# Building the one-hot matrices of an edge aggregation on VectorE (one equality compare) instead of ScalarE (distance and ramp)

## What is computed

```python
msgs = concatenate([h[src], edge_attr_64], axis=-1)     # 100000 x (256 + 64)
msgs = silu(msgs @ W + b)                               # W: 320 x 256
out = segment_sum(msgs, dst, num_segments=3125)         # sum of the messages of each node
out = layernorm(out, eps=1e-3) * gamma + beta
x = x + out
```

## Time and profile before

| | |
|---|---|
| median of 3 executions | 7204.5 us |
| the profiled execution | 7204.5 us, span 7202.7 us |
| mean granted clock of TensorE | 0.81 of full speed |
| busy share of the span: PE, PEld, DVE, ACT, POOL | 67%, 49%, 71%, 55%, 68% |
| the stage of the change | about 4826 to 5862 us of the span |

### The profile page before, as it was taken

The page is one execution under the profiler, slowest core; times in us unless marked ns, Lnnn a source line. Parts: engine busy times, 40 slices in busy tenths (PEclk is TensorE's granted clock), DMA queues, the critical chain, the costliest instruction groups (busy, mean ns, idle before and its releaser), DMA issues. The chain is left out here.

```text
span 7202.7 us, 124927 instructions
## 1 busy us (share of the span) xinstructions
PE 4843.2 (67%) x21121; PEld 3517.2 (49%) x21122; DVE 5093.3 (71%) x11748; ACT 3926.9 (55%) x9134; POOL 4916.3 (68%) x4990
## 2 busy tenths in 40 slices
PE   5463157777726777766777777769999971677775
PEld 4353135555514555544555555546666651444443
DVE  7665267777747777787888888875555564777777
ACT  4342157777626777752444444437777751666664
POOL 0376677777567777757777777767777762777773
PEclk9855578888867888888988888879999975778877
DMA  5422244444414444534666666634444432454443
GB/s 175 49 69 46 68 125 136 135 135 136 106 46 135 134 135 136 137 88 133 181 182 176 180 179 179 184 79 131 131 131 131 131 79 69 134 136 137 136 135 86
DMA packets 625331, 906.00 MB, mean 126 GB/s; under 512 B 345945, under 2 KB 399862, under 8 KB 624794
## 3 DMA queue, kind: packets, MB, share of 16 engines
q0 software_dynamic: 248160, 655.67, 33.4%
q1 hardware_dynamic: 376666, 223.78, 12.2%
q10 hardware_dynamic: 416, 25.60, 1.1%
HBM read 869.74 MB, written 61.59 MB: 129 GB/s over the span
## 5 line engine op out<-in xcount | busy, mean ns | idle before, releaser
L1444 POOL DMA_INDIRECT at_ring<-tab_s,at_idx x816 | 774.2, 949 | 310.6 <-issue 204.6
L1924 POOL DMA_INDIRECT ad_ring<-tab_qv,ad_idx x816 | 780.1, 956 | 274.9 <-issue 213.1
L1444 POOL DMA_INDIRECT at_ring_0a<-tab_s,at_idx_0a x816 | 778.4, 954 | 273.5 <-issue 204.5
L1444 POOL DMA_INDIRECT at_ring_0b<-tab_s,at_idx_0b x816 | 777.2, 952 | 273.2 <-issue 205.4
L2305 POOL DMA_INDIRECT ae_ring<-tab_a,ae_idx x816 | 771.3, 945 | 257.6 <-issue 232.9
L1603 PE MATMUL at_po<-at_rows,at_hot 128*128 128x260 f32 x1632 | 562.5, 504 | 109.6 <-DVE at_begin L103 82.3
L2124 PE MATMUL ad_pk<-node_a,ad_hr 128*128 x1632 | 479.4, 445 | 217.4 <-DVE ad_prod L1996 119.1
L1603 PE MATMUL at_po_0b<-at_rows_0b,at_hot_0b 128*128 128x264 f32 x1632 | 510.2, 466 | 113.3 <-DVE at_begin_0b L103 95.9
L1603 PE MATMUL at_po_0a<-at_rows_0a,at_hot_0a 128*128 128x264 f32 x1632 | 505.9, 463 | 114.3 <-DVE at_begin_0a L103 100.4
L575 POOL DMA_INDIRECT recs_s<-rnk_recs_now,rnk_pos_now x294 | 286.6, 975 | 360.3 <-DVE rnk_both L478 272.1
L2199 ACT ACTIVATE ad_hot<-iota_row,ad_nrel 128x128 f32<-128x128 f32 x816 | 259.0, 388 | 487.9 <-PE ad_po L2143 487.9
(11 more groups left out here) (503 smaller groups left out, 12726.9 us busy)
## 6 DMA issues: line engine op xcount, KB each, us to landing
at_rr_0a<-relrow_d SPq DMA_DIRECT2D x102, 256.0 KB
at_rr_0b<-relrow_d SPq DMA_DIRECT2D x102, 256.0 KB
ad_rr<-relrow_d SPq DMA_DIRECT2D x102, 256.0 KB
ae_feat<-attr_pad SPq DMA_DIRECT2D x816, 32.0 KB
at_rr<-relrow_s SPq DMA_DIRECT2D x102, 256.0 KB
rnk_lrow<-lorow_f SPq DMA_DIRECT2D x98, 256.0 KB
attr_pad<-in_edge_attr_dram ACTq DMA_DIRECT2D x1, 25000.0 KB, 79.5
at_ring_0a<-tab_s,at_idx_0a POOLq DMA_INDIRECT x816
```

The source lines that it names most:

```text
L1444: eng.indirect_dma_start(out=ring[:, t.slot * STEP + u, :], out_offset=None, in_=table, in_offset=bass.IndirectOffsetOnAxis(ap=idx[:, t.sl ...
L1924: eng.indirect_dma_start(out=ring[:, t.slot * STEP + u, :], out_offset=None, in_=table, in_offset=bass.IndirectOffsetOnAxis(ap=idx[:, t.sl ...
```

## The change

The one-hot matrices move from ACT to DVE. `prepare(q)` now first issues one `tensor_tensor` with `is_equal` over the quad (128 x 512), whose inputs are `iota_row`, repeated 4 times, and the positions `rel_sb`, each repeated 128 times; both lie in SBUF. ACT's function `one_hots`, its copy of `nrel` and the semaphore `far` are gone, five instructions for each quad and one for each turn. `load_columns` brings `rel` in place of `nrel`. DVE has 24 counted instructions in a turn, before 20, and the counts that PE and ACT wait for follow that; each still stands for the same `pre`. The wait of `add` for `summed` is the same but for an offset.

```diff
-        per = QUAD * 5
-        pre_at = {0: 0, 1: 1, 2: 6, 3: 11}
+        per = QUAD * 6
+        hot_at = {0: 1, 1: 3, 2: 9, 3: 15}
...
                         def silu(q):
-                            eng.wait_ge(vec, i * per + (per + pre_at[q] + 1))
+                            eng.wait_ge(vec, i * per + (per + hot_at[q] + 1))
...
-                        def one_hots(q):
-                            eng.wait_ge(summed, i * STEP + (q * QUAD + QUAD))
-                            for j in range(QUAD):
-                                ins = eng.activation(hot[:, q % 2, j, :], iota_row[:, :], ACT.Abs,
-                                                     bias=nrel[:, q * QUAD + j:q * QUAD + j + 1])
-                            ins.then_inc(far, 1)
-                            eng.wait_ge(far, i * 5 + q + 2)
-                            eng.activation(hot[:, q % 2, :, :], hot[:, q % 2, :, :], ACT.Relu, bias=ones[:, 0:1], scale=-1.0)
-                        eng.activation(nrel[:, :], od["nrel_sb"][:, bass.ds(i * STEP, STEP)], ACT.Copy).then_inc(far, 1)
...
                         def prepare(q):
+                            us = bass.ds(i * STEP + q * QUAD, QUAD)
+                            own(eng.tensor_tensor(
+                                hot[:, q % 2, :, :], iota_row[:, :].rearrange("p (o n) -> p o n", o=1).to_broadcast([P, QUAD, P]),
+                                od["rel_sb"][:, us].rearrange("p (u o) -> p u o", o=1).to_broadcast([P, QUAD, P]),
+                                ALU.is_equal), False)
                             for j in range(QUAD):
                                 eng.wait_ge(landed[q * QUAD + j], i * 16 + 16)
                             eng.wait_ge(mapped, i * 4 + q + 1)
...
-                        eng.wait_ge(vec, i * per + (12, per + 1, per + 2, per + 7)[q])
+                        eng.wait_ge(vec, i * per + (16, per + 2, per + 4, per + 10)[q])
```

More of the change, by code:

```diff
@@ L2248, in _ @@
             def _(eng):
-                eng.dma_start(od["nrel_sb"][:, :], od["nrel"]).then_inc(loaded, 16)
+                eng.dma_start(od["rel_sb"][:, :], od["rel"]).then_inc(loaded, 16)
                 eng.dma_start(od["oth_sb"][:, :], od["oth"]).then_inc(loaded, 16)
@@ L2281, in aggregate_edges @@
             hot = sb(f"ae_hot_{tag}", [P, 2, QUAD, P], F32, c)
-            nrel = sb(f"ae_nrel_{tag}", [P, STEP], F32, c)
             pre = sb(f"ae_pre_{tag}", [P, 2, QUAD, D], F32, c)
@@ L2290, in aggregate_edges @@
             seen, fed = ph.sem("ae_seen"), ph.sem("ae_fed")
-            far = ph.sem("ae_far")
             told, warmed = ph.sem("ae_told"), ph.sem("ae_warmed")
@@ L2344, in silu @@
                         def silu(q):
-                            eng.wait_ge(vec, i * per + (per + pre_at[q] + 1))
+                            eng.wait_ge(vec, i * per + (per + hot_at[q] + 1))
                             eng.activation(msg[:, q % 2, :, :], pre[:, q % 2, :, :], ACT.Silu).then_inc(msgs, 1)
-                        def one_hots(q):
-                            eng.wait_ge(summed, i * STEP + (q * QUAD + QUAD))
-                            for j in range(QUAD):
-                                ins = eng.activation(hot[:, q % 2, j, :], iota_row[:, :], ACT.Abs,
-                                                     bias=nrel[:, q * QUAD + j:q * QUAD + j + 1])
-                            ins.then_inc(far, 1)
-                            eng.wait_ge(far, i * 5 + q + 2)
-                            eng.activation(hot[:, q % 2, :, :], hot[:, q % 2, :, :], ACT.Relu, bias=ones[:, 0:1], scale=-1.0)
-                        eng.activation(nrel[:, :], od["nrel_sb"][:, bass.ds(i * STEP, STEP)], ACT.Copy).then_inc(far, 1)
                         evacuate(0)
                         evacuate(1)
-                        eng.wait_ge(far, i * 5 + 1)
-                        one_hots(0)
                         silu(0)
                         feed(i + 1, 0)
-                        one_hots(1)
                         evacuate(2)
@@ L2368, in _ @@
                         feed(i + 1, 1)
-                        one_hots(2)
                         evacuate(3)
@@ L2372, in _ @@
                         feed(i + 1, 2)
-                        one_hots(3)
                         silu(3)
@@ L2405, in _ @@
                                                     (j % 2) * D:(j % 2 + 1) * D], D,
-                                    lambda u: eng.wait_ge(summed, i * STEP + (u | 1) + 1 + 2 * QUAD))
+                                    lambda u: eng.wait_ge(summed, i * STEP + (u | 1) + 1))
                         prepare(0)
@@ L2421, in _ @@
                     eng.sem_inc(turned, 4)
-                    eng.sem_inc(summed, 2 * QUAD)
                     def turn(i, q):
@@ L2505, in gnn_kernel @@
     with ExitStack() as c:
-        order["d"]["nrel_sb"] = sb("nrel_sb", [P, UP], F32, c)
+        order["d"]["rel_sb"] = sb("rel_sb", [P, UP], F32, c)
         order["d"]["oth_sb"] = sb("oth_sb", [P, UP], U32, c)
```

## The result

The kernel after took 7281.61 us (median of 4, 7274.12 to 7295.61) against 7201.81 for the kernel before in the same comparison: ratio 1.0112, 95% interval [1.0093, 1.0132], some 80 us slower. The forecast was 7228.5 and the range ended at 7258. The direction was right; more than two thirds of the loss were not in the sum.

A forecast was written before the change was run, and what follows sets the result against it. POOL's gathers at 20.0 a turn were taken as the bound, the other engines' chain close behind at 19.80; that chain's +23.7 and the gathers' +24 came out level, so 7204.5 plus 24 gave 7228.5, range 7209 to 7258.

The forecast's parts named there:

- What bounds the kernel: Third layer's stage: POOL's gathers set its length at 20.0 a turn, the other engines' chain hardly shorter at 19.80.
- the second chain: The engines other than POOL in the third layer's stage, waiting on each other in turn: 19.80 for each turn before.
- (a): ACT loses 462 us of busy time in one-hot work; nobody waits for it, so counted as nothing.
- (b): DVE gets 204 compares of 128 x 512, taken as 0.68 each, within 0.61 to 1.222.
- (c): A turn's second, third and fourth compares fit DVE idle times of 2.08 and 0.97, so cost nothing.
- (d): A turn's first compare has no idle time behind the positions' load; prepare(0) and all behind it come 0.4 later.
- (e): PE's clock: a wait longer by 0.4 makes fast turns rarer; turn taken as 20.45, between 20.20 and 20.57.
- the 8.5 of waits for rows: DVE's waits for gathered rows in the second chain's sum, expected to go once that chain comes last.
- the third rival: Clock: the longer wait brings two stretches at 1.2 GHz into each turn, 7305; chance 0.05.
- (f): Compares with two SBUF inputs hold POOL's gathers at their start: 0.125 each on average, 26 for the stage.
- the second rival: Compares meet gathers in a steady pattern: +57, 7262 if half cost 0.56, 7318 if all; chance 0.08.
- both chains level: Gathers at +24 and the other engines' chain at +23.7 come out equal, so either could be the limit.

The follow-up runs named there:

- f2: Kernel before, all gathers, with four spare PE products between project(0) and project(1); ratio 0.9993, turns of 20.00.
- e5: Kernel before with one gather in each quad instead of four, other slots zeroed; 9434.2, ratio 0.9416, mean turn 19.80.
- q1: Kernel before with one gather in each quad and one spare compare ahead of prepare(0) only, ACT still building one-hots; 7232.35, ratio 1.0036.
- e4: Kernel after with one gather in each quad instead of four, other slots zeroed; 9571.96, ratio 0.9519, turns of 20.48.
- e3: Kernel before, all gathers, with spare compares ahead of prepare(1), (2) and (3), none ahead of prepare(0); ratio 1.001.
- n4: e4 plus a DVE memset of 128 x 176 ahead of a turn's first compare; 9657.85, ratio 0.962, turns of 22.0 and 22.4.
- n3: e4 plus four spare PE products between project(0) and project(1); 9494.02, ratio 0.9456, turn of 18.80.
- q2: Kernel after with one gather in each quad and each compare behind its addition instead of ahead; 7231.67, ratio 1.0037, turns of 20.48.

## Why the prediction was right in direction and short in size

**What bounds the kernel** was right: two limits side by side. f2 shows the gathers at 20.0, e5 the second chain at 19.80 with a quarter of the gathers.

**(a)** ACT's freed 7.7 us a turn bought nothing, as said: q1, where ACT still builds the one-hots, has the turn of e4. **(b)** The compare takes 0.685, taken 0.68. **(c)** The other three compares lie in idle times; 0.97 became 0.37, and q1 without them has the turn of e4 with them.

**(d)** The delay of `prepare(0)` behind the load was 0.34 (forecast 0.35 to 0.43). Missed: 0.22 more on the loop's way to the load, which e3 has without any compare ahead of `prepare(0)`. A turn of one slow stretch went from 20.11 to 20.67, by these 0.56. Against 0.40 this is 0.16 x 49 = 8 us. Why the way grew is open; behind the branch there are 0.16 to 0.19 in the quarter kernels and 0.29 as soon as n4 adds one instruction.

**(e)** This is the step that failed. It let the wait of 2.1 grow by 0.4 and took from it only fewer fast turns (20.45 of at most 20.57). "2.5 is not much more" was argued from a mean granted clock of 0.93, with no row at a longer wait. The mean hid that the kernel before already fell into turns of two half-speed stretches, three times (21.61, 21.75, 21.53), in part at its usual wait of 2.10. In fact the fast turns go completely at 2.44 (q1, turns of 20.48, as forecast), and at 2.67 a second half-speed stretch comes in 38 of 50 turns. The parts, as an estimate: at full clock 18.48 became about 19.04 (+0.56; n3 has 18.80 with 0.22 less of delay); what the clock adds went from 19.80 - 18.48 = 1.32 to 21.84 - 19.04 = 2.80 (+1.48). So 49 x 0.56 = 27 and 49 x 1.48 = 73, less the 8.5 of waits for rows that went as forecast, is 92, against 93 in the stage. It is the third rival, which had a chance of 0.05 and 7305. n3 (fill the wait, the loss goes) and n4 (lengthen it by 0.29, 1.7 more) show that the wait is the cause, with a quarter of the gathers; with all of them the fill was not timed on a chip with turns of 20. Its length alone does not fix the clock: q2 at 1.93 has no fast turn left, e5 at 1.96 has 10. The two errors belong together: e4 and q1, whose delay lacks the 0.22, have turns of 20.48, and with those the forecast's own sum gives +25 (49 x 0.03 above its 20.45). One reading in the sum was also too simple: the 8.5 called waits for gathered rows are 7.8 of waits by the row, and the three long turns are in it as well.

The Trainium skill, "TensorE: Matmul & The Clock Gate", section "HAM oscillation — how this bites in real kernels", describes waits that send the engine back to the lower clock in every iteration. The traces agree with the pattern, not in every turn at 2.10 (10 of 50 have no half-speed time) but in every turn at 2.42 and above. The waits of that page are DMA waits of about 3 to 5 us; here waits of 1.9 to 2.7 for VectorE are enough.

**(f)** The mechanism is right to the hundredth (1.43). The size was 0.333 for each compare, because the same compares meet the same gathers in turn after turn: 179 gathers took over 1.0, the 15th of a turn in 46 of 51 turns, the 16th and the 9th in 36 each. That is the locked pattern of the second rival, whose reason (POOL waits for ACT's `feed`, which follows the same chain) fits it but was not tested. It cost nothing here: in the sum 839.3 + 815 x 0.305 = 1088 is the gathers' own length, and the stage had 1109.5 from the first to the last start. But the forecast's "both chains level" was wrong by this: the second chain is last by some 20 us, and mending the clock alone would bring back less than 73 (some 20 if the gathers were held as much, an estimate from these sums).

The Trainium skill, "SBUF — State Buffer", section "Who interferes with whom", also holds, as inferred, that a tensor_tensor takes only the read interface, and that descriptor generation needs the write interface. By that the compares would not hold a gather; the row of 1.43 shows that they do.

No version with all its work beat the kernel before on the chips with turns of 20: f2 ties with it, and the fill and the other order in the kernel after were not timed there.

## What to carry to other kernels

An instruction that a new order puts on the chain between two engines can cost more than its own length if TensorE is what waits at the end of it: here 0.56 of delay became 2.04 a turn. Look at the single turns, not at the mean clock: a kind of turn that comes up three times before the change can be the common one after it. Before moving work to an idle engine, ask which of its instructions has no idle time before it: three of the four compares lay in idle times here, and the turn's first one brought most of the loss. And where a view names as a wait's releaser a tile of another stage, look up when each thing waited for was done before calling it late.

## What was not expected of the hardware

- The clock against the wait ahead of `project(1)`: at 0.38 and 0.70 no half-speed time; at 1.96 and 2.10 in most turns one stretch, in some none or two (3.07 and 2.73 us a turn); at 2.42 to 2.44 one in every turn (3.41); at 2.67 to 2.71 two in most or all (6.14, 6.83). It is not this wait alone: q2 has 1.93 there, 0.68 more ahead of `reduce(3)`, and 3.41 in every turn.
- DVE's loop branch has 0.16 to 0.19 behind it in the kernel before and most quarter kernels, 0.29 in n4 and in every kernel with all gathers and an added compare.
- On some of the chips met the same kernel takes some 10,040 in place of 7,203, at 35 GB/s as at 88, and not because rows land later. There the kernel after with the compare behind the addition is 0.2 to 0.3% faster than before (0.9973, 0.9975, 0.9982), and a spare first compare 0.3 to 0.4% slower. Why is open.
